# Selective scan of a 16-layer kernel: decay factors in PSUM, one 1024-column scan for each state, C read from PSUM

## The reference

```python
x_dbl = x_b @ x_proj_w.T
delta, b, c = jnp.split(x_dbl, [DT_RANK, DT_RANK + D_STATE], axis=-1)
delta = jax.nn.softplus(delta @ dt_proj_w.T + dt_proj_b)
a = -jnp.exp(A_log)
# _selective_scan:
deltaA = jnp.exp(jnp.einsum('bld,dn->bldn', delta, a))
deltaBu = jnp.einsum('bld,bln,bld->bldn', delta, b, u)
def step(h, inp):
    dA_t, dBu_t, c_t = inp
    h = dA_t * h + dBu_t
    y = jnp.einsum('bdn,bn->bd', h, c_t)
    return (h, y)
# then
y = y + x_b * D_param
y = y * jax.nn.silu(res)
return y @ out_proj_w.T + out_proj_b
```

## Time and profile before

| | us |
|---|---|
| median of 3 runs | 4177.59 |
| lowest, highest | 4173.52, 4181.47 |
| the profiled execution's own time | 4174.83 |
| its span in the trace | 4173.0 |
| the scan part in it, from its first matmul (112.9) to its last add (509.6) | 396.7 |

### The profile page before, as it was taken

How to read it: one execution, slowest core, us unless ns; L and a number is a source line. 1 busy time by engine, 2 the same in 40 slices (tenths; PEclk the granted TensorE clock), 3 DMA queues, 4 the chain that set the end, 5 groups by cost and what they waited for, 6 DMA issues and landing times. The chain is left out here.

```text
span 4173.0 us, 66414 instructions
## 1 busy us (share of the span) xinstructions
PE 3548.8 (85%) x25764; PEld 2345.8 (56%) x25764; DVE 2154.9 (52%) x4401; ACT 1512.9 (36%) x3057; POOL 920.8 (22%) x1265
## 2 busy tenths in 40 slices
PE   4667659979599787697989899999699996969997
PEld 1222247756477554565657566666466664746664
DVE  5999754445544666334543323333355553445554
ACT  4333224434244333121522233434244542425453
POOL 0334222223222201001000112222212224512222
PEclk7787779989799877697989778878699997969998
DMA  1000000000000000100100000000112210111221
GB/s 67 0 0 0 33 18 1 1 21 22 1 1 1 1 1 1 52 1 11 26 6 1 1 1 1 0 0 0 42 39 66 66 55 16 27 52 46 67 67 46
DMA packets 37333, 89.81 MB, mean 22 GB/s; under 512 B 3889, under 2 KB 24369, under 8 KB 36273
## 3 DMA queue, kind: packets, MB, share of 16 engines
q1 hardware_dynamic: 37040, 85.84, 6.6%
HBM read 70.09 MB, written 15.73 MB: 21 GB/s over the span
## 5 line engine op out<-in xcount | busy, mean ns | idle before, releaser
L1097 ACT ACTIVATE s_sT<-s_E 128x1024 f32<-128x1024 f32 (+2 forms) x448 | 424.4, 947 | 490.9 <-PE s_E L1032 490.0
L1032 PE MATMUL s_E<-s_qA,s_qk 32*128 32x256 f32 (+2 forms) x3584 | 484.5, 388 | 17.3 <-ACT s_sT L1097 6.1
L1032 PEld LDWEIGHTS s_E<-s_qA,s_qk 32*128 32x128 f32 x3584 | 313.2, 189 | 168.5 <-ACT s_sT L1097 79.0
L1129 DVE TENSOR_REDUCE s_negm<-s_S 128x8 f32<-128x2048 f32 x160 | 366.9, 2293 | 72.6 <-PE s_S L1007 64.1
L731 DVE TENSOR_REDUCE s_negmax<-s_S 128x2 f32<-128x512 f32 x135 | 93.2, 691 | 428.7 <-PE s_S L637 428.5
L1144 DVE TENSOR_TENSOR s_qA<-s_qk,s_X 128x256 f32<-128x256 f32 x224 | 94.3, 421 | 417.0 <-PE s_X L1062 417.0
L1007 PE MATMUL s_S<-s_qk 32*128 32x256 f32 (+2 forms) x3584 | 256.1, 402 | 46.0 <-DMA s_qk<-s_scratch 46.0
L2543 DVE TENSOR_TENSOR_SCAN s0s_hs<-s0s_dA,s0s_dBu 128x256 f32<-128x256 f32 x256 | 282.5, 1164 | 13.8 <-POOL s0s_dBu L2491 6.4
L2459 PE MATMUL s0s_Y<-all_hT,all_ident 128*128 128x512 f32 x256 | 167.5, 790 | 109.4 <-DVE all_hT L2513 85.0
L573 POOL TENSOR_TENSOR s_pr<-s_pr,s_rinv 128x512 f32<-128x512 f32 x134 | 139.3, 1039 | 496.5 <-DVE s_rinv L741 496.4
L1050 PE MATMUL s_OB<-s_sT,s_v 128*32 128x256 f32 (+2 forms) x3584 | 229.4, 375 | 3.9 <-POOL s_sT L1119 1.9
(11 more groups left out here) (577 smaller groups left out, 7189.2 us busy)
## 6 DMA issues: line engine op xcount, KB each, us to landing
s_wB<-enc_b SPq DMA_DIRECT2D x32, 962.5 KB, 4.8
s_scratch<-s_pk SPq DMA_DIRECT2D x56, 256.0 KB, 2.0
s_qk<-s_scratch SPq DMA_DIRECT2D x224, 64.0 KB
s_wA<-enc_a SPq DMA_DIRECT2D x32, 193.0 KB, 4.1
big<-moe SPq DMA_DIRECT2D x2, 2601.0 KB, 11.6
big<-routed SPq DMA_DIRECT2D x2, 2564.0 KB, 12.1
all_W<-weights SPq DMA_DIRECT2D x1, 2552.5 KB, 17.5
all_W<-weights SPq DMA_DIRECT2D x1, 2552.0 KB, 11.9
```

The source lines that it names most:

```text
L1032: last = pe.matmul(b.E[:, i, a.at(kt)], b.qk[rows, r % 2, 1, c, kt * P:(kt + 1) * P], b.qA[rows, u % 2, lo:hi], start=True, stop=True, ski ...
L1097: act.activation(b.sT[:, u % 2, 2 * p:2 * p + 2, 0:a.width], b.E[:, :, 0:a.width], ACT.Exp).then_inc(s.expd, 1)
L1129: ins = dve.tensor_reduce(b.negm[:, u % 2, :, a.HD::32].rearrange("p t h -> p h t"), b.S[:].rearrange("p h (t k) -> p h t k", t=TT), AX_X, ...
```

## The change

What it does, in the scan part alone:

- `dA` moves from SBUF to PSUM (4 banks). The first column of each sequence is set to 0 once, by a memset; the exponentials write only the other 255 columns of each sequence (`segments`).
- The four scans of 256 columns become one of 1024. Where a sequence begins, the factor 0 drops the state that the sequence before left.
- `BC` (4 banks) becomes `BB` (1 bank, B) and `CB` (1 bank, C), with one buffer each. ScalarE copies `BB` alone (512 columns) to `bb` in SBUF, two buffers. `times_c` reads C from `CB`.
- `OUT` goes away. `outputs` writes into `BB`, and the next B spread waits until `add_x` has read it. `add_x` comes two steps earlier in VectorE's loop.
- TensorE's loop is written anew: wait for the copy of q, spread B of q+1, wait for `times_c(q-1)`, spread C of q, sum of step q-1.

```diff
-            dA = ss.sb("dA", [P, 2, M, C])
-            bc = ss.sb("bc", [P, 3, 2, C])
+            bb = ss.sb("bb", [P, 2, C])
...
-            BC = ss.ps("BC", [P, 2, 2, C])
+            dA = ss.ps("dA", [P, 2, M, C])
+            BB = ss.ps("BB", [P, C])
+            CB = ss.ps("CB", [P, C])
             Y = ss.ps("Y", [P, M, C])
-            OUT = ss.ps("OUT", [P, 2, C])
...
+            def segments(t):
+                return t.rearrange("p (b t) -> p b t", b=2)[:, :, 1:]
+
+            def projects(q):
+
+                return q // N - 1 if q % N == 6 and q > N else None
...
+                    def spread(to, q, row, sem):
+                        c = q // N
+                        for k in range(3):
+                            last = pe.matmul(to, g.ident_bf[0:ROWS, row:row + 1].to_broadcast([ROWS, P]),
+                                             xparts[:, k, c * C:(c + 1) * C], start=(k == 0), stop=(k == 2))
+                        last.then_inc(sem, 1)
...
-                    broadcasts(0)
-                    broadcasts(1)
-                    for q in range(Q + 2):
-                        if q + 2 < Q:
-                            broadcasts(q + 2)
-                        if q % N == 6 and q > N:
-                            outputs(q // N - 1)
-                        j = q - 2
+                    spread(BB[:], 0, 32, bb_mm)
+                    for q in range(Q + 1):
+                        if q + 1 < Q:
+                            pe.wait_ge(bb_cp, q + 1)
+                            if (c := projects(q)) is not None:
+                                outputs(c)
+                                pe.wait_ge(added, c + 1)
+                            spread(BB[:], q + 1, 32 + (q + 1) % N, bb_mm)
+                        if q >= 1:
+                            pe.wait_ge(hcs, q)
+                        if q < Q:
+                            spread(CB[:], q, 64 + q % N, cb_mm)
+                        j = q - 1
                         if j < 0:
                             continue
                         first, last_ = j % N == 0, j % N == N - 1
                         if first and j:
                             pe.wait_ge(gated, 2 * (j // N) - 1)
-                        pe.wait_ge(hcs, j + 1)
...
-                        act.wait_ge(bc_mm, q + 1)
-                        if q >= 3:
-                            act.wait_ge(hcs, q - 2)
-                            act.wait_ge(dbu, q - 2)
-                        act.activation(bc[:, q % 3, :, :], BC[:, q % 2, :, :], ACT.Copy).then_inc(bc_cp, 1)
-
+                        act.wait_ge(bb_mm, q + 1)
+                        if q >= 2:
+                            act.wait_ge(dbu, q - 1)
+                        act.activation(bb[:, q % 2, :], BB[:], ACT.Copy).then_inc(bb_cp, 1)
...
                         dve.wait_ge(scans, q + 1)
+                        dve.wait_ge(cb_mm, q + 1)
...
                         dve.tensor_tensor(hc[:, q % 2, :, :], hs[:, q % 2, :, :],
-                                          bc[:, q % 3, 1:2, :].to_broadcast([P, M, C]), ALU.mult).then_inc(hcs, 1)
+                                          CB[:].unsqueeze(1).to_broadcast([P, M, C]), ALU.mult).then_inc(hcs, 1)
...
-                        for m in range(M):
-                            for b in range(2):
-                                cols = slice(b * T, (b + 1) * T)
-                                ins = dve.tensor_tensor_scan(out=hs[:, q % 2, m, cols], data0=dA[:, q % 2, m, cols],
-                                                             data1=dBu[:, q % 2, m, cols], initial=0.0,
-                                                             op0=ALU.mult, op1=ALU.add)
-                        ins.then_inc(scans, 1)
+                        dve.tensor_tensor_scan(out=hs[:, q % 2, :, :].rearrange("p m c -> p (m c)"),
+                                               data0=dA[:, q % 2, :, :].rearrange("p m c -> p (m c)"),
+                                               data1=dBu[:, q % 2, :, :].rearrange("p m c -> p (m c)"), initial=0.0,
+                                               op0=ALU.mult, op1=ALU.add).then_inc(scans, 1)
```

More of the change, by code:

```diff
@@ L2406, in mamba_stage @@
             yv = ss.sb("yv", [P, M, C])
-            BC = ss.ps("BC", [P, 2, 2, C])
+            dA = ss.ps("dA", [P, 2, M, C])
+            BB = ss.ps("BB", [P, C])
+            CB = ss.ps("CB", [P, C])
             Y = ss.ps("Y", [P, M, C])
-            OUT = ss.ps("OUT", [P, 2, C])
-            split, bc_mm, bc_cp, exps, dbu, scans, hcs, summed, gated, out_mm, added = [
-                ss.sem(n) for n in ("split", "bc_mm", "bc_cp", "exps", "dbu", "scans", "hcs", "summed", "gated", "out_mm",
-                                    "added")]
+            split, cleared, bb_mm, bb_cp, cb_mm, exps, dbu, scans, hcs, summed, gated, out_mm, added = [
+                ss.sem(n) for n in ("split", "cleared", "bb_mm", "bb_cp", "cb_mm", "exps", "dbu", "scans", "hcs",
+                                    "summed", "gated", "out_mm", "added")]
             Q = NC_ * N
+            def segments(t):
+                return t.rearrange("p (b t) -> p b t", b=2)[:, :, 1:]
+            def projects(q):
+                return q // N - 1 if q % N == 6 and q > N else None
             with nc.Block() as block:
@@ L2416, in _ @@
                 def _(pe):
[L2417 to L2428, removed]
+                    def spread(to, q, row, sem):
[4 more added lines that the diff above has]
+                        last.then_inc(sem, 1)
                     def outputs(c):
                         pe.wait_ge(gated, 2 * (c + 1))
-                        if c >= 2:
-                            pe.wait_ge(added, c - 1)
                         for t in range(4):
-                            o = OUT[:, c % 2, t * P:(t + 1) * P]
+                            o = BB[:, t * P:(t + 1) * P]
                             for m in range(M):
@@ L2465, in copy @@
                     def copy(q):
-                        act.wait_ge(bc_mm, q + 1)
-                        if q >= 3:
-                            act.wait_ge(hcs, q - 2)
-                            act.wait_ge(dbu, q - 2)
-                        act.activation(bc[:, q % 3, :, :], BC[:, q % 2, :, :], ACT.Copy).then_inc(bc_cp, 1)
+                        act.wait_ge(bb_mm, q + 1)
+                        if q >= 2:
+                            act.wait_ge(dbu, q - 1)
+                        act.activation(bb[:, q % 2, :], BB[:], ACT.Copy).then_inc(bb_cp, 1)
+                    act.wait_ge(cleared, 1)
                     copy(0)
@@ L2477, in _ @@
                         for m in range(M):
-                            ins = act.activation(dA[:, q % 2, m, :], delta[:, m, c * C:(c + 1) * C], ACT.Exp,
-                                                 scale=aneg[:, m * N + n:m * N + n + 1])
+                            ins = act.activation(segments(dA[:, q % 2, m, :]), segments(delta[:, m, c * C:(c + 1) * C]),
+                                                 ACT.Exp, scale=aneg[:, m * N + n:m * N + n + 1])
                         ins.then_inc(exps, 1)
@@ L2487, in _ @@
                         c = q // N
-                        pool.wait_ge(bc_cp, q + 1)
+                        pool.wait_ge(bb_cp, q + 1)
                         if q >= 2:
@@ L2491, in _ @@
                         pool.tensor_tensor(dBu[:, q % 2, :, :], du[:, :, c * C:(c + 1) * C],
-                                           bc[:, q % 3, 0:1, :].to_broadcast([P, M, C]), ALU.mult).then_inc(dbu, 1)
+                                           bb[:, q % 2, :].unsqueeze(1).to_broadcast([P, M, C]), ALU.mult)\
+                            .then_inc(dbu, 1)
                 @block.vector
                 def _(dve):
+                    dve.memset(dA[:].rearrange("p i m c -> p (i m) c")[:, :, 0::T], 0.0).then_inc(cleared, 1)
                     x2 = xd[0:ROWS, :]
@@ L2531, in add_x @@
                         xt = g.x[:, 4 * c:4 * c + 4, :]
-                        dve.tensor_tensor(xt, xt, OUT[:, c % 2, :].rearrange("p (t d) -> p t d", t=4), ALU.add)\
+                        dve.tensor_tensor(xt, xt, BB[:].rearrange("p (t d) -> p t d", t=4), ALU.add)\
                            .then_inc(added, 1)
@@ L2550, in _ @@
                             finish(q // N - 1)
-                        if q % N == 8 and q > N:
-                            add_x(q // N - 1)
+                        if (c := projects(q)) is not None:
+                            add_x(c)
                     times_c(Q - 1)
```

## The result

| | median, us | lowest to highest | runs |
|---|---|---|---|
| before | 4174.14 | 4165.78 to 4184.51 | 14 |
| changed | 4191.34 | 4186.29 to 4207.58 | 14 |

The ratio is 1.0043, with a 95% interval of 1.0033 to 1.0054: the change makes the kernel slower by 17.2 us, or 0.43%. A second series gave 1.0048 (1.0030 to 1.0067; medians 4196.78 and 4176.28). The scan part in it lasts from 115.1 to 542.6: 427.5 us, where it was 396.6 (112.91 to 509.55; the rounded ends give 396.7).

A forecast was written before the change was run, and what follows sets the result against it. VectorE was taken to bound the scan part before, the ring after. 31.5 turns x 12.0 = 378, plus 26, is 404 against 366.4 (+37.6); head -6: +31.6 on 4174.83, 4206.4, plus 2.8: 4209 us, range 4160 to 4245.

The forecast's parts named there:

- The stall goes: VectorE's scans no longer stand still until GpSimd's multiply finishes, as `dA` is read from PSUM: 2.1 us a step saved.
- The long scan: On VectorE, one scan of 1024 columns replaces four of 256 and takes 2.17 us, within bounds 2.0 and 2.66.
- a turn: One round of the ring, covering two scan steps: 11.9 to 12.0 us, 6.0 a step.
- PSUM inputs at nothing: VectorE's reading of inputs from PSUM costs nothing extra; the skill's fixed cycles would add 0.065 us on scan and `times_c` each.
- The ring: TensorE's B spread, ScalarE's copy, GpSimd's `dBu`, scan, `times_c`, back to TensorE: cannot overlap itself, 6.7 us without x.
- x: TensorE's ten records in the ring (3 C, 4 of the sum of a step, 3 B): 5.2 us, mostly at low clock.
- The chunk ends: At the three chunk ends, `finish` adds 4.2 us and the projection with `add_x` 4.5: 26 us together.
- The sum: Scan part's middle: 31.5 turns x 12.0 = 378, plus 26, is 404 us against 366.4; with the head, +31.6 in all.
- The head: From the first matmul to the end of the first `times_c`: 16.4 us before, 10.4 after, so -6.
- the tail: End of the scan part, after the middle: the same work, 0 us change.
- the last step, from the profiled execution to the median: The median of the whole kernel's runs lies 2.8 us above the profiled execution: 4206.4 becomes 4209 us.

## Why the prediction was right

4209 us were forecast, and slower (chance 0.70); 4191.34 were measured, inside 4160 to 4245, slower by 0.43% where 0.75% was forecast. Step by step:

- **The stall goes.** Right: no scan or multiply is stretched in the changed kernel, and the experiment with the factors in SBUF brings it back.
- **The long scan.** 2.17 us was taken and 2.29 measured. I had taken the fixed part of an add (0.15 us) for a scan; from 256 columns (0.656) to 1024 (2.29) a column costs 2.13 ns and not 1.97. That is 0.12 us a turn, 4 us in all.
- **PSUM inputs at nothing.** Right: the scan takes 2.29 us with the factors in PSUM and in SBUF, `times_c` 1.20 and 1.19. The prediction had worked out an estimate of 0.065 us on each from the fixed cycles that the Trainium skill gives (VectorE: DVE Perf Modes, "The TRN2 errata"); neither instruction shows it.
- **The ring.** Right in every member: alternating steps of 3.53 and 8 to 9 us; the wait of VectorE for GpSimd every second step, 158.3 us over 31 times, 5.1 each, where about 5 was given. TensorE's idle stretch is 3.60 us, as summed. Without x a turn has 6.8 us (the three matmuls of B are through at 167.11, the next group begins at 173.89), where 6.7 was summed; the longer scan is the difference.
- **x, TensorE's ten records.** Taken at 5.2, as a value between two means. They last from 149.88 to 154.57, from 161.34 to 167.11 and from 173.89 to 178.51: 4.7, 5.8 and 4.6 us. The two sizes alternate, so the mean is 5.2, and a turn 11.9. The mean granted clock is 0.77. The reason given holds: of the 32 groups that begin after a wait, 29 do so at 1.2 GHz (1.46 us for the three matmuls of C; 1.13 us in the other three). But nothing in the prediction told of two sizes, and why they alternate is open; that their mean falls on 5.2 is in part luck.
- **The chunk ends.** Mis-sized by a little: steps of about 13.0 at each `finish` and 14.1 at each projection, against a mean long step of 8.4. That is 3 x (4.6 + 5.7) = 31 us, where 26 were taken; the projection was the dearer one.
- **The sum** for the middle was 404 us, and 403.9 were measured. That close an agreement is luck: the chunk ends took 5 us more than summed, and all else in the middle 373 us (403.9 less 31) instead of 378. The head gave back 6.1 us (16.5 to 10.4) where 6 were taken, the tail 0.6 where none was. For the whole scan part +31.6 was summed, and +30.9 measured (427.5 less 396.6).

**What was mis-sized** is the last step, from the profiled execution to the median. It added 2.8 us, the distance of before's profile from the median of its first 3 runs (over 14 runs it is -0.7). The changed kernel's profiled execution lies 16 us above its own median, at the upper end of its runs, so 4209 fits the profile (4207.58) and is 18 us above the median. The scan part itself held in three profiles (427.5, 427.4, 426.6) and in the medians of the kernels with one layer (+28.5); why the whole kernel's median rose by only 17 to 21 us is open. The text gave no width for that step.

## What to carry to other kernels

When a change frees the engine that bounds a stage, write down each remaining engine's queue in order and look for a ring: a single buffer whose refill stands in an in-order queue behind work that waits for the ring's own last member. Its turn is the sum of all members, however idle each of them is. Here it showed as a constant time for two steps, in most of the runs split into a short and a long one. Moving three matmuls ahead of one wait turned a loss of 0.4% into a gain of 3.3%.

TensorE's time after an idle stretch is not its time in a full queue: here 4.6 to 5.8 us against 3.0 for the same ten records. Take it from rows that begin after such a stretch.

## What the runs showed of the hardware

- Adding matmuls can make a kernel faster: 6 zero matmuls a step raised the mean granted clock from 0.77 to 0.95, and took 57 us off a stretch of 427.
- The exclusion of VectorE and GpSimd works both ways and passes along. In the kernel before with the long scan, GpSimd waited about 1.0 us for a scan that was under way, and VectorE's next instruction waited 2.1 us for GpSimd.
- ScalarE's exponentials of 510 columns into PSUM took 0.68 us each; into SBUF, in the experiment with the factors there, 0.71. They are off the ring, and no engine's wait is put down to them in the changed kernel.
